# A two-layer AdaLN transformer on one core: the first stage in another order, and row maxima, products and lead rearranged in layer 1's attention

## What is computed

```python
mod = (silu(c) @ wmod).reshape(2, 6, 1, 256)
sa, ca, ga = mod[:, 0], mod[:, 1], mod[:, 2]
ga = (2 * (ga >= 0) - 1) * maximum(abs(ga), 0.25)
h = layernorm(x) * (1 + ca) + sa
# layer 0: q, k, v = h @ W + b, 8 causal blocks wide, one head of 256
x = x + ga * attention(h)
# layer 1: 16 heads of 16
scores = where(causal, -inf, einsum('bhqd,bhkd->bhqk', q, k))
attn = softmax(scores / sqrt(16))
ctx = einsum('bhqk,bhkd->bhqd', attn, v)
x = x + ga * (ctx @ W_out + b_out)
```

## Time and profile before

| | us |
|---|---|
| median of 3 runs | 1415.04 |
| lowest and highest | 1408.33, 1415.26 |
| the profiled execution | 1416.65 |
| its span | 1414.9 |
| PE, DVE, ACT, POOL busy | 1267.6, 808.3, 587.3, 470.7 |
| mean granted clock of PE | 0.948 |

### The profile page before, as it was taken

The page is one execution under the profiler, slowest core; times in us unless marked ns, Lnnn a source line. Parts: engine busy times, 40 slices in busy tenths (PEclk is TensorE's granted clock), DMA queues, the critical chain, the costliest instruction groups (busy, mean ns, idle before and its releaser), DMA issues. The chain is left out here.

```text
span 1414.9 us, 18305 instructions
## 1 busy us (share of the span) xinstructions
PE 1267.6 (90%) x5944; PEld 870.4 (62%) x5944; DVE 808.3 (57%) x1733; ACT 587.3 (42%) x1089; POOL 470.7 (33%) x335
## 2 busy tenths in 40 slices
PE   4999769999999999999998969888888668999897
PEld 4866658888888778888886622222222236778665
DVE  4455554444444444444446577777768274978565
ACT  1321233333333433333333516666666443443553
POOL 2200225555555555555554321111111023422000
PEclk9999759999999999999999978999999987999899
DMA  4010123333334344334430450222211301110001
GB/s 146 1 45 1 58 70 106 118 116 104 104 113 119 89 110 115 104 104 117 113 97 1 156 160 6 66 78 68 76 20 24 90 0 35 34 56 23 1 15 45
DMA packets 49308, 102.67 MB, mean 73 GB/s; under 512 B 8660, under 2 KB 21716, under 8 KB 49244
## 3 DMA queue, kind: packets, MB, share of 16 engines
q1 hardware_dynamic: 49244, 101.87, 25.1%
HBM read 88.52 MB, written 8.93 MB: 69 GB/s over the span
## 5 line engine op out<-in xcount | busy, mean ns | idle before, releaser
L921 DVE TENSOR_TENSOR d_prod<-d_silu,ps 128x512 f32<-128x512 f32 x132 | 90.8, 688 | 247.6 <-ACT d_silu L872 244.6
L1417 DVE CUSTOM_DVE_ANT_0 masked<-ps,causal 128x128 f32<-128x128 f32 (+7 forms) x256 | 184.0, 756 | 60.5 <-PE ps L1237 58.4
L970 POOL TENSOR_TENSOR d_inter<-d_prod,d_wbc 128x512 f32<-128x512 f32 x132 | 199.3, 1523 | 21.4 <-DVE d_prod L921 15.0
L960 POOL TENSOR_TENSOR d_w_lo<-raw,d_w_hi 128x768 fp32r<-128x768 f32 x66 | 122.2, 1852 | 229.2 <-ACT d_w_hi L848 229.2
L913 DVE TENSOR_TENSOR d_i_lo<-d_inter,d_i_hi 128x512 fp32r<-128x512 f32 x132 | 155.1, 1175 | 64.2 <-ACT d_i_hi L854 64.2
L776 PE MATMUL ps<-h_hi,d_w_hi 128*128 128x512 f32 x528 | 167.0, 397 | 5.4 <-POOL d_w_lo L960 4.5
L776 PE MATMUL ps<-h_lo,d_w_hi 128*128 128x512 f32 x528 | 166.4, 395 | 0.0
L776 PE MATMUL ps<-h_hi,d_w_lo 128*128 128x512 f32 x528 | 166.0, 395 | 0.0
L1397 ACT ACTIVATE xn<-ps 128x512 f32<-128x512 f32 (+3 forms) x256 | 116.2, 509 | 71.3 <-PE ps L1257 67.7
L848 ACT CAST d_w_hi<-raw 128x768 fp32r<-128x768 f32 x66 | 54.9, 833 | 198.7 <-PE ps L789 197.0
L776 PEld LDWEIGHTS ps<-h_hi,d_w_hi 128*128 128x128 f32 x528 | 99.1, 188 | 29.9 <-POOL d_w_lo L960 5.8
(11 more groups left out here) (248 smaller groups left out, 2146.0 us busy)
## 6 DMA issues: line engine op xcount, KB each, us to landing
d_wbc<-router_weights_t SPq DMA_DIRECT2D x132, 256.0 KB, 3.8
raw<-in_moe SPq DMA_DIRECT2D x66, 384.0 KB, 4.1
qk<-qk_parts SPq DMA_DIRECT2D x72, 128.0 KB, 2.7
qk_parts<-parts SPq DMA_DIRECT2D x16, 384.0 KB, 2.6
raw<-in_mlp SPq DMA_DIRECT2D x16, 384.0 KB, 3.1
h_t<-qk_parts SPq DMA_DIRECT2D x24, 128.0 KB, 2.7
x_tok<-in_x SPq DMA_DIRECT2D x4, 512.0 KB, 8.3
h_hi<-raw SPq DMA_DIRECT2D x32, 64.0 KB, 2.3
```

What stands on the lines that cost most here:

```text
L921: nc.vector.tensor_tensor(prod[:, s % 3, :], sg[:, s % 3, :], ps[:, 2 * (s % 2) + 1, :], ALU.mult).then_inc(s_t, 1)
L960: nc.gpsimd.tensor_tensor(w_lo[:, slot, :], raw[:, slot, :], w_hi[:, slot, :].bitcast(F32), ALU.subtract).then_inc(s_wlo, 1)
L970: nc.gpsimd.tensor_tensor(inter[:, s % 3, :], prod[:, s % 3, :], wbc[:, s // 2, (s % 2) * GW:(s % 2 + 1) * GW], ALU.mult).then_inc(s_int, 1)
L1417: nc.vector.tensor_tensor_reduce(masked[:, at % 2, 0:k], ps[:, bank:bank + 2, :].rearrange("p a n -> p (a n)")[:, 0:k], causal[:, SEQ - k: ...
```

## The change

In the first stage: the modulation columns go to bank 6 and signal by themselves; PE's transposes of group 0 come before the gate rows, which go to bank 7, and PE no longer waits for the finished modulation; DVE normalises group 0 right behind its own statistics, finishes the modulation next, and then does group 1 and the gate rows; the bf16 cast of the constants comes last, and v's first products wait for it; in the loop DVE normalises group g + 2, not g + 1, ahead of the evictions of group g. POOL takes the weights' low part before the power of group 1, and each group's low h before the power of group g + 2.

In layer 1's attention: the products of groups 2 and 3 (j = 8 to 15) are issued by halves, one half behind each of the entries 2 to 17; their remainders follow on DVE behind entries 6, 8, ... 20; `EARLY` is 2 instead of 5; `due` gets up to `LEAD` = 9 entries more, growing over the twelve blocks of pass 0 and staying. The memset of the ones beside v comes behind remainder 7 instead of 3.

```diff
--- before.py
+++ after.py
@@ -297,24 +297,25 @@
                     for b in range(BATCH):
                         last = nc.vector.tensor_copy(crep[:, b], bc(csilu[:, 0, :, b], 2, P))
                     last.then_inc(s_crep, 1)
+                    dve.wait_ge(s_x[0], 16)
+                    ln_stats(0, link)
+                    ln_rows(dve, 0, s_ln, 0)
+                    dve.wait_ge(s_modp, 1)
+                    mod_finish(0, link, ps[:, 6, 0:24], (0,)).then_inc(s_modd, 1)
+                    dve.wait_ge(s_x[1], 16)
+                    ln_stats(1, link)
+                    ln_rows(dve, 1, s_ln, 0)
+                    dve.wait_ge(s_modp, 2)
+                    link(nc.vector.tensor_copy(ga[:, :, :], ps[:, 7, :].rearrange("p (b d) -> p b d", b=BATCH)))
+                    guard(ga[:, :, :], (gat[:, 0], gat[:, 1]), link)
                     dve.wait_ge(s_const, 16)
                     nc.vector.tensor_copy(cbf[:, :], consts[:, 0:384]).then_inc(s_cb, 1)
-                    dve.wait_ge(s_x[0], 16)
-                    ln_stats(0, link)
-                    dve.wait_ge(s_x[1], 16)
-                    ln_stats(1, link)
-                    ln_rows(dve, 0, s_ln, 0)
-                    dve.wait_ge(s_modp, 1)
-                    link(nc.vector.tensor_copy(ga[:, :, :], ps[:, 1, :].rearrange("p (b d) -> p b d", b=BATCH)))
-                    guard(ga[:, :, :], (gat[:, 0], gat[:, 1]), link)
-                    mod_finish(0, link, ps[:, 0, 0:24], (0,)).then_inc(s_modd, 1)
                     dve.wait_ge(s_bias, 48)
                     for g in range(NG):
                         if g + 2 < NG:
                             dve.wait_ge(s_x[g + 2], 16)
                             ln_stats(g + 2, link)
-                        if g + 1 < NG:
-                            ln_rows(dve, g + 1, s_ln, 0)
+                            ln_rows(dve, g + 2, s_ln, 0)
                         for m in range(KC):
                             dve.wait_ge(s_proj, 6 * g + 2 + m + 1)
                             nc.vector.tensor_scalar(kt[:, m, g * GW:(g + 1) * GW], ps[:, 4 + m, :],
@@ -324,39 +325,39 @@
                             nc.vector.tensor_copy(vtok[:, 4 * g + 2 * m:4 * g + 2 * m + 2, :],
                                                   ps[:, 6 + m, :].rearrange("p (t d) -> p t d", t=2))\
                                 .then_inc(s_pev_d, 1)
-                    dve.wait_ge(s_modp, 2)
+                    dve.wait_ge(s_modp, 3)
                     mod_finish(0, link, ps[:, 0, 0:24], (1,))
 
                 @block.gpsimd
                 def _(pool):
                     nc.gpsimd.memset(half[:, :], -0.5).then_inc(s_half, 1)
                     pool.wait_ge(s_half, 1)
-                    ln_pool(pool, 0, range(2))
+                    ln_pool(pool, 0, range(1))
                     pool.wait_ge(s_whi, 1)
                     nc.gpsimd.tensor_tensor(wq_lo[:, :, :, :], wqkv[:, :, :, :], wq_hi[:, :, :, :].bitcast(F32),
                                             ALU.subtract).then_inc(s_wlo, 1)
+                    ln_pool(pool, 0, (1,))
                     for g in range(NG):
+                        low_h(pool, g, s_h).then_inc(s_hlo, 1)
                         if g + 2 < NG:
                             ln_pool(pool, 0, (g + 2,))
-                        low_h(pool, g, s_h).then_inc(s_hlo, 1)
 
                 @block.tensor
                 def _(pe):
                     pe.wait_ge(s_csilu, 1)
                     pe.wait_ge(s_wmods[0], 16)
-                    mod_columns(0, wmod, ps[:, 0, 0:24], range(6))
+                    mod_columns(0, wmod, ps[:, 6, 0:24], range(6)).then_inc(s_modp, 1)
+                    pe.wait_ge(s_const, 16)
+                    pe.wait_ge(s_ln, 1)
+                    ln_transposes(0, 0).then_inc(s_lnt, 1)
                     pe.wait_ge(s_crep, 1)
                     for b in range(BATCH):
                         for k in range(KC):
-                            last = nc.tensor.matmul(ps[:, 1, b * D:(b + 1) * D], crep[:, b, k, :],
+                            last = nc.tensor.matmul(ps[:, 7, b * D:(b + 1) * D], crep[:, b, k, :],
                                                     wmod[:, k, GATE_A * D:(GATE_A + 1) * D], start=k == 0, stop=k == KC - 1)
                     last.then_inc(s_modp, 1)
-                    pe.wait_ge(s_modd, 1)
-                    pe.wait_ge(s_const, 16)
                     pe.wait_ge(s_wqkv, 48)
                     pe.wait_ge(s_wlo, 1)
-                    pe.wait_ge(s_ln, 1)
-                    ln_transposes(0, 0).then_inc(s_lnt, 1)
                     for g in range(NG):
                         pe.wait_ge(s_h, g + 1)
                         for w in range(2):
@@ -383,6 +384,8 @@
                         for m in range(2):
                             if g:
                                 pe.wait_ge(s_pev_d, 4 * (g - 1) + 2 + m + 1)
+                            else:
+                                pe.wait_ge(s_cb, 1)
                             for i in range(2):
                                 t = 4 * g + 2 * m + i
                                 for n, (h, wt) in enumerate(((h_hi, wq_hi), (h_hi, wq_lo), (h_lo, wq_hi))):
@@ -1091,7 +1094,7 @@
                 NTI = len(tiles)
                 STEPS = NTI * HQ
                 LAG = 2
-                EARLY, LATE_ROWS = 5, 3
+                EARLY, LATE_ROWS, LEAD = 2, 3, 9
 
                 entries = []
                 for v in range(NV + 1):
@@ -1102,8 +1105,8 @@
                             entries.append((v - 1, HQ * TB))
                 place = {e: n for n, e in enumerate(entries)}
                 ahead = place[0, HQ * TB] + 1 + EARLY
-                due = [min(len(entries), ahead + (at * 3 + min(h, 2) + 1) * (HQ * TB + 1) // (3 * NTI))
-                       for at in range(NV * NTI) for h in range(HQ)]
+                due = [min(len(entries), ahead + (at * 3 + min(h, 2) + 1) * (HQ * TB + 1) // (3 * NTI)
+                           + min(LEAD, at * LEAD // NTI)) for at in range(NV * NTI) for h in range(HQ)]
 
                 p_pre = xn[:, :, :].rearrange("p (r a) d -> p r (a d)", a=2)
                 p_post = rzb0[:, :, :].rearrange("p k (r n) -> p (k r) n", n=GW)
@@ -1129,11 +1132,16 @@
 
                 s_bank = [0, 6]
                 ST, AV = 2, 5
-                LAST = NG - 1
-
-                def parts_between(at):
-
-                    return [4 * LAST + at // 4 - 2] if at in (8, 12, 16, 20) else []
+
+                def product_at(at):
+
+                    n = at - 2
+                    return (8 + n // 2, n % 2) if 0 <= n < 16 else None
+
+                def remainder_at(at):
+
+                    n = at - 6
+                    return 8 + n // 2 if 0 <= n < 16 and n % 2 == 0 else None
 
                 def width(n):
                     g, j = tiles[n]
@@ -1283,17 +1291,17 @@
                                 pe.wait_ge(s_h, g - 1)
                             ln_transposes(g, 0).then_inc(s_lnt, 1)
 
-                        def projected(g, w, m):
-
-                            j = 4 * g + 2 * w + m
-                            if g and j % 4 == 0:
+                        def product(j, k):
+
+                            g, w, m = j // 4, (j // 2) % 2, j % 2
+                            if k == 0 and g and j % 4 == 0:
                                 pe.wait_ge(s_h, g)
-                            if g:
+                            if k == 0 and g:
                                 pe.wait_ge(s_rest, j - 3)
-                            for k in range(KC):
-                                last = nc.tensor.matmul(ps[:, 2 + j % 4, :], wqkv1[:, w, k, m * P:(m + 1) * P],
-                                                        h_t[:, k, g * GW:(g + 1) * GW], start=k == 0, stop=k == KC - 1)
-                            last.then_inc(s_proj, 1)
+                            ins = nc.tensor.matmul(ps[:, 2 + j % 4, :], wqkv1[:, w, k, m * P:(m + 1) * P],
+                                                   h_t[:, k, g * GW:(g + 1) * GW], start=k == 0, stop=k == KC - 1)
+                            if k == KC - 1:
+                                ins.then_inc(s_proj, 1)
 
                         def valued(g):
 
@@ -1310,20 +1318,19 @@
                                                                 start=k == 0, stop=k == KC - 1)
                                 last.then_inc(s_vp, 1)
 
-                        for g in range(NG - 1):
-                            if g < GB:
-                                transposed(g + 1)
-                            if g == GB:
-                                transposed(NG - 1)
-                                for n in range(NG):
-                                    valued(n)
-                            for j in range(4):
-                                projected(g, j // 2, j % 2)
+                        for g in range(GB):
+                            transposed(g + 1)
```

(19 more changed lines are left out.)

## The result

The median after is 1390.01 us (1385.89 to 1392.53, four runs), against 1413.98 for the kernel before beside it (four runs). The ratio is 0.9838 with a 95% interval of [0.981, 0.9866]: 24.0 us or 1.7% faster by the medians, clear of the noise. The profiled execution took 1390.41 us, its span is 1388.7 against 1414.9, 26.2 us less. The forecast was 1385 with a range from 1376 to 1399. Direction and range held; the gain in the profiled execution is 26.2 us, where the sum said 30.7.

What follows compares the result with a forecast made beforehand. PE, busy for 90% of the span, was taken as the bound. First stage 14.0, ahead of the exponentials 6.9 and passes 9.8 sum to 30.7 us off 1416.65: 1386.0, median 1.6 lower, so 1385; range 1376 to 1399.

Steps and rivals of the forecast that it cites:

- The clock term: First stage, group 0: with PE's gaps gone, half-rate products speed up, taken as 1.9 of 2.9 us.
- 1 us of room: First stage: k's evictions begin near 28.8 and PE needs the bank near 29.8, leaving 1 us.
- Rival four: First stage: gate rows' later guard blocks evictions, group 1 stalls 3 to 4 us, total 1389; 0.19 together with rival two.
- Ahead of the exponentials: Layer 1's attention before pass 0: spread products let PE start at 844.2 instead of 851.08, 6.9 us, bounds 0 and 9.
- the count of its queue: SP before pass 0: stores of parts 12 to 15 and twelve loads each for passes 1 and 2 end near 841.
- rival two: Ahead of the exponentials: cold seam, four to eight slow halves cost 3.5 to 7 us; 0.19 together with rival four.
- the six: Pass boundaries: PE's six waits for the rows of maxima all go through the lead, 9.9 us.
- the price of the nine entries: Pass 0: 42 entries instead of 33 cost 2.7 us if PE bears them, 6.8 if DVE; taken as 3.4.
- 1.5 for the clock: Passes: two low-clock stretches of 5 us at boundaries cost 3 us, of which 1.5 was taken as gain.
- 1.8 for fewer entries: Last passes: six fewer entries give 1.8 us, bounds 0 and 4.5.
- Rival one: Passes: another wait replaces that for the rows, so the lead buys nothing, total 1395; chance 0.17.
- Rival three: Passes, from 844 on: finer spreading keeps PE thin and the clock low, 39 us cost, total 1425; chance 0.02.

Runs made afterwards that it cites:

- The two edits: Changed kernel with POOL's low part waiting for DVE's rows: 1387.63 us; changed kernel with k's evictions ahead of the rows of group g + 2: 1393.96 us.
- rows first: Changed kernel with the DMA of pass 0's rows of maxima ahead of the loads for pass 2, wo and bo on SP's queue: 1386.15 us.
- no lead: Changed kernel with EARLY 5 and LEAD 0, products still spread singly: 1400.64 us.
- the combined one: Changed kernel with pass 0's rows DMA ahead on SP, POOL's low part waiting for DVE's rows, EARLY 5 and LEAD 6: 1382.54 us, ratio 0.9794.
- rows after k: Changed kernel with DVE evicting group g's k ahead of normalising the rows of group g + 2: 1393.96 us.
- the lead of six: Changed kernel with LEAD 6 instead of 9, EARLY still 2: 1394.55 us.
- The first half alone: First stage of the changed kernel with everything behind it from the kernel before: 1404.27 us, ratio 0.9922 to before.

## Why the prediction was right or wrong

**First stage, 14.0 forecast, 11.9 measured.** Group 0 was forecast at 18.5 and came at 18.58, 10.2 of the 10.3 us; the step that carried it, the modulation held by POOL's subtraction and done at 15.6, came at 15.65. The clock term, inside group 0, was put at 1.9 of 2.9. The products with high h took 3.81 us (18.58 to 22.39) where before took 6.59 (28.77 to 35.36), so 2.8 came back; the 24 two-column products did not keep the rate low here. The granted clock reads 1.00 in both traces at this place, so this is read from durations alone. The rule of the Trainium skill that the prediction named (TensorE: Matmul & The Clock Gate, "What's actually happening"), by which all 2.9 come back, was nearer than the 1.9. Group 0 as a whole gained only 2.3 (12.16 to 9.88), because the change put a new wait in it: PE stands for the cast of the constants before v's first products, 0.4 us counted against group 2. The prediction had the cast end near 24 and PE ask at 25. It ended at 25.48, since DVE's normalisations of group 1 had been held for 3.44 us and the gate copy began at 22.03. With POOL made to wait this loss is gone too. Group 1 was to gain 1.8 and lost 0.6 (11.15 to 11.74), a miss of 2.4, which is more than the whole of the stage's.

The step that failed is "1 us of room" at k's bank. It took the four normalisations of group 2 at their free 1.38 us. The prediction knew from the earlier trace rows that DVE is held by POOL and applied it to the modulation, but not to these four, which it had itself put beside POOL's low part by its new order. They took 3.43 and PE stood 2.18 us. The Trainium skill (SBUF — State Buffer, "Who interferes with whom") says that tensor_scalar on SBUF can take both port pairs and that whichever of DVE and GpSimd starts second is blocked for the whole instruction. The trace agrees (3.43 against 1.38, all of the difference in the first of the four), and applying it to each tensor_scalar on SBUF beside a POOL row would have found the 2 us. Rival four named the stall with another place and 3 to 4 us. The two edits show the cause: from the start of group 0 to the columns it takes 39.35 us in after, 36.95 without the overlap and 36.92 with the hold but nothing behind it. Either way 2.4 us come back, as much as group 1's miss.

**Ahead of the exponentials, 6.9 forecast, 5.0 measured.** The spreading works as described and is worth 5.3 us by itself. Two terms were too small. SP: the count of its queue put its end near 841, at the same time as the rows of maxima, 36 us behind the first maximum. It came at 38.4, behind four stores and twelve loads that wait for their data, and wo and bo, which the count left out. The copy of the rows began at 34.8, so the DVE chain was, if anything, shorter than forecast. Moving the one DMA forward gave 3.3 us. The clock: rival two in small. It had four to eight halves at the low level; there were two, and 1.7 us. Its cause is half settled. Filling the gap kept the clock up in the one profile taken, but the kernels "rows first" and "no lead" had the same gap (1.40 and 1.37 us ahead of the first maximum, 1.36 in after) and stayed at the high level. So the gap alone doesn't bring the fall; what decides it from one execution to the next was not found.

**The passes, 9.8 forecast, 10.2 measured,** by errors that cancel. Waits: the six were to give 9.9 us and did, shown by their return when the lead is taken away; passes 1 to 5 gave 8.9 against their five waits' 8.4, and the steady pass, forecast at 31 to 31.5, is 31.2.

Pass 0 was to be 36 to 38 and took 40.70. The step that failed is the price of the nine entries, taken at 3.4 us as nearer PE's 2.7 than DVE's 6.8. They cost 6.1, nearly DVE's price: 0.68 each against a mean maximum of 0.756. DVE's "about as much room as they need" was no room. What three of them cost was measured twice and differs: 2.3 us between this kernel and the combined one, 0.95 between "rows after k" and the lead of six, which both have the long low stretch. The low level also lasts 12 us from the start of pass 0 against 9.8 in before; "no lead", with the same 12, is only 0.5 us longer in pass 0 than before.

At the end it was the other way: 1.5 for the clock and 1.8 for fewer entries were forecast, 6.4 us came, 5.1 of it in pass 6 (35.71 to 30.60). The step that was too small there is the clock. In before it was low twice in this pass, for 6.8 us from 1052.1 and for 3.4 us from 1082.8. The first half alone, whose passes have the text of before, fell only once in it, for 3.4 us, and took 33.15, so the long stretch cost some 2.6 us. With the new lead one low stretch of 3.4 us in pass 6 makes it 31.75 to 32.07 instead of 30.60, 1.2 to 1.5 more. Taken together, as an estimate: 3.9 of the 5.1 are the clock and 1.2 the fewer entries. The clock's part is in part luck, for it fell in pass 6 in four of the ten profiles with the new lead. The other stretch that the prediction counted, at 953 to 956, lay in pass 3 (33.89).

Rival one (another wait takes over) was wrong: nothing did. Rival three, the slow side, was wrong: the low level did reach back before pass 0, but the clock is 1.00 from 848 on.

**The sum.** 11.9 - 0.9 + 5.0 + 10.2 = 26.2 against 30.7. The miss is 2.1 in the first stage, 1.9 at the head, 0.9 of drift in unchanged code, less 0.4 in the passes, where 2.7 too much was hoped for in pass 0 and the clock at the end gave more than was counted on. The direction and the mechanism of the three parts held; that the passes' sum is so near is luck.

## What to carry to other kernels

When an instruction of POOL is moved, lay it beside DVE's instructions on SBUF (those seen held here are all tensor_scalars), and price each that falls in it at POOL's end, together with what is queued behind it. When work ahead of a critical DMA gets shorter, count the issuing queue to the last entry, by when each entry's data is there, since that queue is the next bound. A lead that removes a wait at every boundary is paid once, in the first pass, at the price of its dearest engine; make it as small as the longest wait asks, and put what you can of it into the idle time ahead of that pass.

## What was not expected of the hardware

- A DVE instruction on four elements per partition is held for as long as a large one: 1.85 us instead of 0.17, to the end of POOL's 3.43 us subtraction. Of four instructions in a row the first alone is held (2.46 and 2.36 us, then 0.40 each), and it is enough that POOL started its low part 0.07 and 0.17 us earlier.
- The low level at the beginning of pass 0 lasted about 12 us in most profiles of the new attention and 17.6 and 17.7 in two, one of them with that part's text unchanged, with PE busy for 3.92 and 4.00 of 4 us in the stretches where it lasted. The six extra microseconds cost 1.5.
- Two neighbouring kernels with the same gap of 1.4 us ahead of the first maximum kept the clock, in seven other profiles, the changed kernel's two among them, it fell to 1.2 GHz; the fall cost 1.7 us. Behind the stall of 2.18 us in the first stage it fell in three profiles of seven and cost 1.5.
